# A mixture-of-experts kernel in float32: the second expert product with the gelu outputs as the stationary operand

## The reference

```python
x = x + 0.5 * ffn(layernorm(x), gate_w, w1, w2)
x = x + attention(layernorm(x), Wq, Wk, Wv, Wo, head_scales, head_dirs)
x = x + 0.5 * ffn(layernorm(x), gate_w, w1, w2)

# ffn: 16 experts, top-1 routing, capacity 320 tokens an expert, w1 16x128x512, w2 16x512x128
dispatch = einsum('sec,sd->ecd', sec_mask, tokens)
h = gelu(einsum('ecd,edf->ecf', dispatch, w1))
expert_out = einsum('ecf,efd->ecd', h, w2)
out = einsum('sec,ecd->sd', combine_weights, expert_out)
```

## Time and profile before

| | us |
|---|---|
| median of 3 runs | 639.26 |
| lowest and highest | 638.13, 642.31 |
| span of the profiled execution, first to last instruction | 637.1 |
| the profiled execution's own time | not among the listed ones; 2.2 around its span would make it the median |
| TensorE busy | 512.4 (80%) |
| VectorE, ScalarE, GpSimd busy | 350.6, 317.2, 222.6 |

### The profile page before, as it was taken

How to read it: one execution, slowest core, us unless ns; L and a number is a source line. 1 busy time by engine, 2 the same in 40 slices (tenths; PEclk the granted TensorE clock), 3 DMA queues, 4 the chain that set the end, 5 groups by cost and what they waited for, 6 DMA issues and landing times.

```text
span 637.1 us, 11661 instructions
## 1 busy us (share of the span) xinstructions
PE 512.4 (80%) x3083; PEld 372.8 (59%) x3083; DVE 350.6 (55%) x1826; ACT 317.2 (50%) x624; POOL 222.6 (35%) x266
## 2 busy tenths in 40 slices
PE   3554589999265999999899899999999955999980
PEld 2443366666034677776677667777776732766650
DVE  3576124332269758869779687876856242233330
ACT  3344134343045576767667667666666431444430
POOL 2577205455424310504205242142030332053563
PEclk9999999999695799999999999999999966999995
DMA  7711544544234000000000000000000012455420
GB/s 248 217 43 49 192 121 150 171 149 155 73 98 173 1 3 0 18 2 18 10 8 16 17 16 4 14 18 19 18 18 18 16 31 58 139 161 163 151 84 17
DMA packets 44832, 45.82 MB, mean 72 GB/s; under 512 B 4935, under 2 KB 34016, under 8 KB 44760
## 3 DMA queue, kind: packets, MB, share of 16 engines
q1 hardware_dynamic: 40184, 37.13, 19.1%
q0 software_dynamic: 4608, 8.22, 3.7%
HBM read 29.61 MB, written 19.17 MB: 77 GB/s over the span
## 4 chain that ended last, share of the span: by engine, by line
PE 57%; DVE 15%; issue 9%; DMA 6%; POOL 5%; ACT 3%; another core or an unknown queue 2%; SPq 1%; DVEq 0%; POOLq 0%; ACTq 0%
PE b L774 12%; PE sc L605 10%; PE b L615 6%; DVE junk L1190 4%; PE b L594 4%; PE sc L739 3%; PE sc L713 3%; PE sc L742 3%; PE b L781 2%; DMA rows<-slots 2%; POOL slots L1339 2%; PE b L685 2%; PE b L629 2%; POOL out L1360 2%
## 5 line engine op out<-in xcount | busy, mean ns | idle before, releaser
L774 PE MATMUL b<-probs,vaug 128*128 128x256 f32 x448 | 107.5, 380 | 0.0
L774 PEld LDWEIGHTS b<-probs,vaug 128*128 128x128 f32 x448 | 81.6, 194 | 8.9
L1190 DVE CUSTOM_DVE_ANT_0 junk<-sc,cht 128x256 bf16<-128x256 f32 (+1 forms) x256 | 82.2, 387 | 8.4 <-PE sc L713 7.2
L1385 POOL COPY vaug<-vall 128x64 f32<-128x64 f32 (+1 forms) x32 | 7.8, 248 | 206.0 <-PE b L781 130.9
L1339 POOL DMA_INDIRECT slots<-pay,slot_i x64 | 63.5, 992 | 41.8 <-issue 20.3
L914 ACT ACTIVATE hT<-sc 128x320 f32<-128x320 f32 x128 | 56.0, 437 | 44.2 <-PE sc L605 33.2
L605 PE MATMUL sc<-enT,w1s 128*128 128x320 f32 x256 | 74.8, 436 | 0.8 <-DVE enT L1153 0.4
L615 PE MATMUL b<-hT,w2s 128*128 128x320 f32 x256 | 73.8, 433 | 0.0
L978 ACT ACTIVATE probs<-sc 128x1024 f32<-128x1024 f32 x48 | 49.2, 1025 | 21.9 <-PE sc L742 21.0
L605 PEld LDWEIGHTS sc<-enT,w1s 128*128 128x128 f32 x256 | 47.5, 190 | 21.3 <-issue 3.2
L1360 POOL DMA_INDIRECT x<-yrow,ytok x40 | 39.0, 975 | 59.8 <-DVE yrow L1163 48.9
(11 more groups left out here) (143 smaller groups left out, 963.4 us busy)
## 6 DMA issues: line engine op xcount, KB each, us to landing
w1s<-in_L_ffn_w SPq DMA_DIRECT2D x32, 256.0 KB
w2s<-in_L_ffn_w SPq DMA_DIRECT2D x32, 256.0 KB
slots<-fresh SPq DMA_DIRECT2D x16, 330.0 KB, 4.5
rows<-slots SPq DMA_DIRECT2D x16, 330.0 KB
xall<-in_L_attn_x SPq DMA_DIRECT2D x8, 256.0 KB
xall<-x SPq DMA_DIRECT2D x8, 256.0 KB, 2.8
out<-xall SPq DMA_DIRECT2D x8, 256.0 KB, 2.3
slots<-pay,slot_i POOLq DMA_INDIRECT x64
```

What stands on the lines that cost most here:

```text
L774: last = mm(b5[:, 0:G * P], vcols[:, t - 1 + kb, P * j:P * (j + 1)], probs[t % 2][:, j, kb].rearrange("p g q -> p (g q)"), start=(j == 0 a ...
L1190: ins = v.tensor_tensor_reduce(junk[:, H // 2 * h + i, lo:], sc[h][:, i // G, 2 * P * (i % G) + lo:2 * P * (i % G + 1)], tab16["window"][: ...
```

## The change

The second product is turned round. For each of the 5 tiles c, `hT[a][:, f, 64 columns of tile c]` is stationary and `w2s[a][:, f, :]`, 128 columns, moves. The result of expert 0 goes to output partitions 0 to 63 and that of expert 1 to 64 to 127 of the same 128 columns of a bank, so tokens stand on partitions. In the built program the matmuls of a = 0 sit in array columns 0 to 63 and those of a = 1 in 64 to 127. The transposes back, `yT`, `y_copy` and their semaphores go; `add_back` reads the new tiles `ytile` in b6 and b7. One semaphore, `e_down`, takes the place of the four. VectorE's step now has `add_back(p-1)` between `norm(p+1)` and `copy_in(p+1)`, and TensorE's down(p) waits for `add_back(p-1)` (`e_rows`), since `ytile` is single.

```diff
-        yps = [b6[:, 0:CAP], b7[:, 0:CAP]]
+        ytile = [b6[:, P * c:P * (c + 1)] if c < 4 else b7[:, 0:P] for c in range(PC)]
...
-                        sp.wait_ge(e_yps[1], g)
+                        sp.wait_ge(e_down, g)
                         sp.dma_start(w2s[1][:], w2_e[bass.ds(p * 2 + 1, 1)].rearrange("e p c d -> (e p) c d")).then_inc(w2_in[1], 16)
...
-                    sp.wait_ge(e_yps[0], g + 1)
+                    sp.wait_ge(e_down, g + 1)
                     sp.dma_start(w2s[0][:], w2_e[bass.ds(nxt, 1)].rearrange("e p c d -> (e p) c d")).then_inc(w2_in[0], 16)
...
-                    wait(pe, e_rows, (max(g - 2, g0) if isinstance(p, int) else g - 2) * PC)
+                    wait(pe, e_xT, g)
...
-                def down(p, a):
-                    g = p + g0
-                    pe.wait_ge(w2_in[a], (g + 1) * 16)
-
-                    wait(pe, e_yT[a], g)
-                    for f in range(FC):
-                        pe.wait_ge(e_gelu, (g * 2 + a) * FC + f + 1)
-                        last = mm(yps[a], w2s[a][:, f, :], hT[a][:, f, :], start=(f == 0), stop=(f == FC - 1))
-                    last.then_inc(e_yps[a], 1)
-
-                def turn_back(p):
+                def down(p):
                     g = p + g0
                     for a in range(2):
-                        pe.wait_ge(e_yT[a], g + 1)
...
+                        pe.wait_ge(w2_in[a], (g + 1) * 16)
+                    pe.wait_ge(e_gelu, (g + 1) * 2 * FC)
+
+                    wait(pe, e_rows, g * PC)
                     for c in range(PC):
-                        last = turn(b4[:, P * c:P * (c + 1)] if c < 4 else b5[:, 0:P], yT[:, c, :], ident)
-                    last.then_inc(e_back, 1)
+                        for f in range(FC):
+                            for a in range(2):
+                                last = mm(ytile[c][HALF * a:HALF * (a + 1)], hT[a][:, f, HALF * c:HALF * (c + 1)], w2s[a][:, f, :],
+                                          start=(f == 0), stop=(f == FC - 1))
+                    last.then_inc(e_down, 1)
...
-                    wait(act, e_yps[a], g)
...
+                    wait(act, e_down, g)
...
-                    dve.wait_ge(e_back, g + 1)
+                    dve.wait_ge(e_down, g + 1)
...
                     if has(p + 1, PAIRS):
                         norm(p + 1)
+                    if has(p - 1, PAIRS):
+
+                        add_back(p - 1, (u + 1) % 2, j + (u - 1) + g0 // 2)
+                    if has(p + 1, PAIRS):
                         copy_in(p + 1)
-                    if has(p - 1, PAIRS):
-
-                        add_back(p - 1, (u + 1) % 2, j + (u - 1) + g0 // 2)
```

More of the change, by code:

```diff
@@ L231, in macaron @@
         hT = [sb(f"hT{i}", [P, FC, CAP]) for i in range(2)]
-        yT = sb("yT", [P, PC, P])
         yrow = [sb(f"yrow{i}", [P, PC, D]) for i in range(2)]
@@ L326, in macaron @@
         e_gelu = sem("e_gelu")
-        e_yps = [sem("e_yps0"), sem("e_yps1")]
-        e_yT = [sem("e_yT0"), sem("e_yT1")]
-        e_back = sem("e_back")
+        e_down = sem("e_down")
         e_rows = sem("e_rows")
@@ L510, in experts @@
                 if phase == 0:
-                    sp.wait_ge(e_yps[1], PAIRS)
+                    sp.wait_ge(e_down, PAIRS)
                     sp.dma_start(w2s[1][:], w2_e[1]).then_inc(w2_in[1], 16)
@@ L634, in step @@
                         up(p, 0)
-                    if has(p - 1, PAIRS):
-                        down(p - 1, 1)
-                    if has(p, PAIRS):
                         up(p, 1)
@@ L643, in step @@
                             warm(3)
-                    elif has(p, PAIRS):
-                        turn_back(p - 1)
                     if has(p, PAIRS):
-                        down(p, 0)
-                    if has(p - 1, PAIRS) and not (isinstance(p, int) and p == PAIRS - 1):
-                        turn_back(p - 1)
+                        down(p)
                 pe.wait_ge(scattered[1 - phase], 16 * TB * (4 + 8 * phase))
                 warm(8)
-                sweep(pe, step, -1, E_LO, E_HI, PAIRS + 1)
+                sweep(pe, step, -1, E_LO, E_HI, PAIRS)
             bank4.drain(pe, 0)
@@ L665, in _ @@
             pe.wait_ge(e_rows, PAIRS * PC)
-            for a in range(2):
-                pe.wait_ge(e_yT[a], PAIRS)
             pe.wait_ge(weights_in, 16 * N_WEIGHTS)
@@ L906, in experts, with step @@
                 nc.scalar.activation(ready[:, phase:phase + 1], tab["ident"][:, 0:1], ACT.Gelu_apprx_tanh)
-                def gelus(p, a):
+                def step(p):
                     g = p + g0
-                    wait(act, e_yps[a], g)
[L912 to L932, removed]
+                    wait(act, e_down, g)
+                    for a in range(2):
+                        for f in range(FC):
+                            act.wait_ge(e_hid, (g * 2 + a) * FC + f + 1)
+                            nc.scalar.activation(hT[a][:, f, :], hid[f], ACT.Gelu_apprx_tanh).then_inc(e_gelu, 1)
+                sweep(act, step, 0, E_LO, E_HI, PAIRS)
             experts(0)
@@ L1160, in add_back @@
                     v.tensor_copy(ytok[u][:, :], r[:, :, TOKEN])
-                    dve.wait_ge(e_back, g + 1)
+                    dve.wait_ge(e_down, g + 1)
                     for c in range(PC):
-                        v.scalar_tensor_tensor(yrow[u][:, c, :], b4[:, P * c:P * (c + 1)] if c < 4 else b5[:, 0:P],
+                        v.scalar_tensor_tensor(yrow[u][:, c, :], ytile[c],
                                                r[:, c, WEIGHT:WEIGHT + 1], r[:, c, 0:D], ALU.mult, ALU.add).then_inc(e_rows, 1)
@@ L1168, in step @@
                         norm(p + 1)
-                        copy_in(p + 1)
                     if has(p - 1, PAIRS):
                         add_back(p - 1, (u + 1) % 2, j + (u - 1) + g0 // 2)
+                    if has(p + 1, PAIRS):
+                        copy_in(p + 1)
                 sweep2(dve, step, -1, E2_LO, E2_HI, PAIRS + 1)
```

4 lines of the change are left out of this document (removed).

## The result

The changed kernel took 701.8 us (median of 4 runs, 698.7 to 703.9), the kernel before 640.4 beside it. The ratio is 1.095 with a 95% interval of 1.091 to 1.099. I had forecast 663, so the time went up by 61 us where I had +24.

A forecast was written before the change was run, and what follows sets the result against it. It took TensorE to bound the expert step at 10.3 us. W 7.7 plus D 4.7 makes 12.4 a step, +12.0 us a part; 637.1 + 24 = 661, with 2.2 from span to median 663 us, range 652 to 738.

The forecast's parts named there:

- +24: Both expert parts together: forecast added time, +12.0 us in each part.
- W: Expert step, from a second product's end to the next down's start: 7.7 us, bounds 7.1 to 8.4.
- the chain that was named: Between second products: `e_down` releases `w2s[0]`, then `rows`, `en`, `yrow`, then the next down; 7.7 us in all.
- T: Moment a pair's second product is complete (`e_down`); `en` was forecast 4.5 us after it, `yrow` done at 7.6.
- Overlap of the halves: Second product: matmuls in the two column halves overlap fully, loads bound, 0.056 us an instruction.
- D: Duration of the turned second product, 80 instructions: 4.7 us taken, 8.9 if the halves do not overlap.
- partial overlap: Rival for the second product: halves overlap in part, 0.082 us an instruction, 6.75 us, total 696; chance 0.17.
- none: Rival for the second product: halves do not overlap, 0.109 us an instruction, 8.9 us, total 730; chance 0.27.
- open loads: Rival for the second product: loads not hidden under the other half's stream, 0.165 us each, total 801; chance 0.03.
- rival (f): Expert steps: TensorE's idling brings half clock, 6.5 us a step, a third of fourteen steps, +30, total 693; chance 0.05.
- Rival (e): Expert steps: `rows` comes early enough, wait falls to 5.1 us, step 9.8, total 632, faster than before; chance 0.03.
- (a): Main forecast for both expert parts: halves overlap fully, step 12.4 us, total 663, own range 652 to 671; chance 0.42.

The follow-up runs named there:

- the filled kernel: Changed kernel with five unused matmuls of constants in each loop step, between the turn in and the wait for `e_rows`; 654.4 us, ratio 1.051.
- rows early: Changed kernel with the load of `rows` for pair p+2 issued ahead of the wait for `e_down`; 619.7 and 619.8 us, ratios 0.995 and 0.996.

## Why the prediction was right or wrong

- **W**, 7.7 us: right. Measured 7.3 to 8.2 on the first chip and 7.4 to 8.2 on the second, by the chain that was named, link by link. With the clock held up it makes steps of 12.5 against 12.4, and where `rows` comes early W is 5.1 against the 5.1 of the rival. `yrow` started behind `en` and not at T, `en` 4.9 after T, and the down was released by `yrow`.
- **Overlap of the halves**, D = 4.7: right wherever the clock is full and the instructions are there, 4.59. The rivals with partial overlap, none, and open loads are out by the pitch of 0.055. That the first result lies near the 696 of the first of them is chance.
- **The step that failed** is the one that put the same D = 4.7 into every step (8 x 4.7 a part in the sum) and said "the clock at 1.00 throughout the parts". In the loop steps D measured 7.54 in the mean of the first part on the first chip and 5.9 to 7.5 on the second, for two different reasons.
- **On the first chip**, the one of the result, it is the gaps: +34 of the +61. They stand in all twelve loop steps and in neither part's first product, which stands ahead of the loop. The six steps at full clock take 7.3 to 7.5, and the six with a stretch at the lower level hardly more, so the clock explains next to nothing of this miss. What causes the gaps stays open. For a supply of instructions that falls behind: they stand after 59 to 72 instructions, in the loop steps, the profile shows no wait, where the clock is low they are shorter, and the kernel before loses time between instructions in its loop on that chip too. Against a supply that is fetched from memory at that moment: the trace's transfers on its instruction queues near the first part start at 60.8, 86.3, 125.5 and 185.2 us, so five of the six products with gaps have none beside them. The Trainium skill, "TensorE: Matmul & The Clock Gate", Part 2 ("Back-to-back issue gap"), gives TensorE a window of 64 instructions; a window filled during W and used up in the product would come near those counts only if it held matmuls alone, since each of the 80 has a load beside it, and no run here tests it. Against the scatters and the loop no run could decide, since none met that chip again.
- **On the second chip** it is the clock. I had the mechanism, as rival (f): "TensorE now idles some 1.7 us in each step". I gave it 0.05 and a third of the steps; all twelve loop steps had it on the second chip, and nine on the third. I had the price wrong the other way: 6.5 us for a whole step at the lower level, where only a stretch of the product ran at it and cost 1.3 to 2.9. On the second chip it is 19.5 of the 50.5 us, shown by filling TensorE.
- The reading that misled me was a pair of windows in the earlier trace rows: 8.77 of 13.7 us busy was followed by the lower level, and 9.5 of 12.4 seemed enough more. The earlier trace rows has nothing between that 64% and the expert part's 96%, and that was a reason for a larger chance, not for a small one.
- **The base.** My 10.3 us for the step before holds on the first chip; in the trace of the second it is 9.71, and on the two others the kernel before takes the same time within 1.1 us. By that base the +24 is +31, which is what the filled kernel shows.
- **Rival (e)**, faster, was a rival about when `rows` arrives. Its price looks nearly right: 632 for 639, ratio 0.989, and measured 0.995 once the load was issued early. But it is right by other means: the forecast won 0.5 us a step over the 10.3 of the first chip, and against 9.71 a loop step wins nothing. The 3 us come from the rest of the parts: from a part's first product to its last scatter the second run of rows early, on the third chip, has 84.5 us against 87.4 in the trace of before on the second chip, and in the second part 84.3 against 85.2. The changed kernel as it stands never came near its condition.
- **A slip in the sums.** The bounds of W give 663 - 8 = 655 and not 652 as the low end of the forecast's own range, and neither is near the kernel before, so the corner of (a) could not have come out as no change.

## What to carry to other kernels

When a change merges two steps into one, look at what was queued behind the first of them: here a load behind `e_yps[0]` came to stand behind `e_down`, and moving it ahead of that wait took 50 us off the changed kernel on the one chip where both ran, and the change had cost 48 there. When a change makes TensorE wait in each step, price the wait twice, once as idle time and once as a lower clock for the work that follows it. Take the length of small matmuls from a trace for the steps in which their engine has just waited, and not only for the first.

## What was unexpected of the hardware

Float32 matmuls of 64 stationary and 128 moving columns in alternate halves follow one another every 0.055 us, with a fresh load each; in runs of eight in one half, every 0.067. Five matmuls without use, 1.3 us of work in a step of 12.5, took 19.5 us off a kernel. The same two kernels take 640 and 702 us on one chip and 622 to 623 and 670 to 674 on others, and what differs most is time between the instructions of the loop, of a cause that stays open: gaps of 0.16 to 0.94 us in TensorE's stream of the changed kernel, and 1.3 to 1.5 us ahead of VectorE's copy to `enT` in the one before. Where such gaps stand, a stretch at the lower clock cost nearly nothing more.
